# Query and key parts stored in the order of the stacks' rows by eight writes, and the attention maxima spread over experts 3 to 7

## The reference

```python
xn = _layernorm(x)
# L1 attention, 16 heads of 8
att = einsum('bhqd,bhkd->bhqk', q, k) / sqrt(8)
att = softmax(att)                      # needs the maximum of each row
out = einsum('bhqk,bhkd->bhqd', att, v) @ Wo.T + bo
# L1 mixture of experts: 8 experts (top 2 by a router) and a shared one
h = (x @ W1[e]) * silu(x @ W3[e]);  expert_out = h @ W2[e]
out = sum_e expert_out * w_full[e] + shared(x)
x = x + attention + experts
```

## Time and profile before

| | us |
|---|---|
| median of 3 runs | 2470.44 (2469.55 to 2471.82) |
| the profiled execution | 2469.61 |
| its span, first to last instruction | 2467.8 |
| PE busy | 1954.3 (79%) |
| DVE busy | 1303.0 (53%) |
| ACT busy | 731.4 (30%) |
| POOL busy | 309.3 (13%) |
| mean granted PE clock | 0.878 of full |

### The profile page before, as it was taken

How to read it: one execution, slowest core, us unless ns; L and a number is a source line. 1 busy time by engine, 2 the same in 40 slices (tenths; PEclk the granted TensorE clock), 3 DMA queues, 4 the chain that set the end, 5 groups by cost and what they waited for, 6 DMA issues and landing times.

```text
span 2467.8 us, 46598 instructions
## 1 busy us (share of the span) xinstructions
PE 1954.3 (79%) x19644; PEld 1120.4 (45%) x19644; DVE 1303.0 (53%) x3084; ACT 731.4 (30%) x1321; POOL 309.3 (13%) x242
## 2 busy tenths in 40 slices
PE   1887788778888788877888768888688877878777
PEld 1444444444454444534445435454344553445544
DVE  1555455554455554655546455555455554565544
ACT  0222242223522235122251232422233223423133
POOL 0110101102101021011110111101111102011020
PEclk9898898888988799878899789997899978989789
DMA  4000200002000020000200001000110002000010
GB/s 154 1 1 1 44 7 2 1 1 44 7 2 1 1 44 7 2 1 3 43 6 2 1 20 26 6 2 1 30 16 6 2 1 41 5 6 1 1 39 7
DMA packets 33762, 36.08 MB, mean 15 GB/s; under 512 B 3652, under 2 KB 32116, under 8 KB 33012
## 3 DMA queue, kind: packets, MB, share of 16 engines
q1 hardware_dynamic: 33556, 33.10, 6.2%
HBM read 24.44 MB, written 8.65 MB: 13 GB/s over the span
## 4 chain that ended last, share of the span: by engine, by line
PE 61%; DVE 26%; ACT 7%; issue 4%; POOL 1%; DMA 1%; SPq 1%; ACTq 0%; DVEq 0%
PE bank L831 6%; PE bank L846 5%; DVE amx L1428 5%; PE bank L935 4%; PE bank L657 4%; PE bank L856 3%; PE bank L563 3%; PE bank L691 3%; PE bank L603 3%; DVE lrec L1275 3%; DVE lmx L1261 2%; PE bank L796 2%; PE bank L678 2%; PE bank L614 2%; DVE fp L1214 2%
## 5 line engine op out<-in xcount | busy, mean ns | idle before, releaser
L1419 DVE TENSOR_TENSOR mh<-bank,silu 128x512 f32<-128x512 f32 x144 | 98.8, 690 | 232.2 <-PE bank L846 232.2
L1275 DVE RECIPROCAL lrec<-bank 128x256 f32<-128x256 f32 x64 | 112.3, 1755 | 144.0 <-PE bank L704 143.4
L441 POOL TENSOR_TENSOR lc<-lc,ls 128x512 f32<-128x512 f32 x32 | 41.0, 1280 | 1026.6 <-DVE lc L1236 1026.6
L1065 ACT ACTIVATE silu<-bank 128x512 f32<-128x512 f32 x144 | 85.1, 597 | 277.8 <-PE bank L831 277.8
L831 PE MATMUL bank<-xn2T,w_mw 128*128 128x512 f32 x288 | 164.8, 702 | 1.8
L1428 DVE TENSOR_REDUCE amx<-bank 128x2 f32<-128x512 f32 x256 | 155.0, 680 | 0.0
L603 PE MATMUL bank<-hT,w_wqkv 128*128 128x512 f32 x256 | 133.9, 666 | 23.5 <-ACT hT L967 17.3
L856 PEld LDWEIGHTS bank<-w_mw,mh 128*128 128x128 f32 x1152 | 136.7, 192 | 24.2 <-issue 24.2
L856 PE MATMUL bank<-w_mw,mh 128*128 128x128 f32 x1152 | 141.4, 277 | 0.0
L1261 DVE TENSOR_REDUCE lmx<-bank 128x4 f32<-128x512 f32 x128 | 79.5, 684 | 73.8 <-PE bank L657 73.8
L1016 ACT ACTIVATE lnmT<-bank 128x512 bf16<-128x512 bf16 x16 | 9.6, 597 | 348.2 <-PE bank L666 348.2
(11 more groups left out here) (260 smaller groups left out, 3821.9 us busy)
## 6 DMA issues: line engine op xcount, KB each, us to landing
dparts<-parts SPq DMA_DIRECT2D x8, 768.0 KB, 3.6
phi<-dparts SPq DMA_DIRECT2D x96, 64.0 KB
lc<-dparts SPq DMA_DIRECT2D x96, 64.0 KB
w_mw<-in_mw SPq DMA_DIRECT2D x3, 1152.0 KB
x_in<-in_x SPq DMA_DIRECT2D x8, 256.0 KB, 13.7
out<-res SPq DMA_DIRECT2D x8, 256.0 KB, 2.3
w_wqkv<-in_wqkv SPq DMA_DIRECT2D x1, 1536.0 KB
w_w<-in_w SPq DMA_DIRECT2D x1, 682.0 KB
```

The lines of the kernel that those rows point to most:

```text
L1275: V.reciprocal(lrec[:, k % 2, :], bank_of("loc_den", k)[:, 0:SEQ]).then_inc(sem["loc_rec"], 1)
L1419: V.tensor_tensor(mh[:, n % 4, :], bank_of("moe_u", n)[:], silu[:, n % 2, :], ALU.mult).then_inc(sem["moe_h"], 1)
```

## The change

Two edits.

First, `dparts` in device memory has the axes `[w, part, odd, d, h // 2, t]` instead of `[w, part, h, d, t]`. One part of one parity of heads is then one run of 64 KB in the order in which it goes into the stack: 8 rows (d) of 8 KB. The 24 reads keep their place, number and size, each with 8 runs of 8 KB where it had 64 runs of 1 KB. The write is cut into eight, one per pair of heads, each of 16 partitions x 6 runs of 1 KB, and SP waits for all eight (8 * 16 on the semaphore).

Second, `MAX_AT` spreads the 16 pairs over experts 3 to 7 as 2, 3, 3, 4, 4 instead of 5, 5, 6 over experts 5 to 7. The wait for the stacks moves with pair 0 from expert 5 to expert 3. Numbers of later lines grow by one.

```diff
-    "parts_out": 16, "stack_in": 26 * 16, "nm_out": 16, "nm_in": 32,
+    "parts_out": 8 * 16, "stack_in": 26 * 16, "nm_out": 16, "nm_in": 32,
...
-        dparts = nc.dram_tensor("dparts", [2, 3, AH, AD, T], BF16, kind="Internal").ap()
+        dparts = nc.dram_tensor("dparts", [2, 3, 2, AD, AH // 2, T], BF16, kind="Internal").ap()
...
-        MAX_AT = {5: range(0, 5), 6: range(5, 10), 7: range(10, 16)}
+        MAX_AT = {3: range(0, 2), 4: range(2, 5), 5: range(5, 8), 6: range(8, 12), 7: range(12, 16)}
...
-                sp.dma_start(dparts.rearrange("w s h d t -> (h d) w s t"), parts[:]).then_inc(sem["parts_out"], 16)
-                sp.wait_ge(sem["parts_out"], now("parts_out", 16))
+                for h in range(AH // 2):
+                    sp.dma_start(dparts[:, :, :, :, h, :].rearrange("w s o d t -> (o d) (w s) t"),
+                                 parts[2 * AD * h:2 * AD * h + 2 * AD].rearrange("p w s t -> p (w s) t")).then_inc(
+                                     sem["parts_out"], 16)
+                sp.wait_ge(sem["parts_out"], now("parts_out", 8 * 16))
...
-                            sp.dma_start(st_[r0:r0 + AD, :, :],
-                                         dparts[w_, part].rearrange("(h o) d t -> o d h t", o=2)[odd]).then_inc(
-                                             sem["stack_in"], 16)
+                            sp.dma_start(st_[r0:r0 + AD, :, :], dparts[w_, part, odd]).then_inc(sem["stack_in"], 16)
```

## The result

| | before | changed |
|---|---|---|
| median, us | 2470.96 (2469.55 to 2471.82, 4 runs) | 2515.28 (2513.64 to 2522.01, 4 runs) |
| ratio, 95% interval | | 1.019 (1.0178 to 1.0203) |
| the profiled execution, us | 2469.61 | 2522.01, span 2520.2 |

The changed kernel is 44 us slower, 5.5 us a turn. Its profiled execution is the longest of the four, 52 us or 6.6 us a turn above before, so what is read from it is a little more than what the median holds.

What follows compares the result with a forecast made beforehand. PE led the chain, with DVE the bound in experts with maxima. Per turn, 4.35 us wait plus 1.8 clock less 3.5 from maxima gave +2.65, +21 in eight turns: 2492 us, range 2442 to 2540.

Steps and rivals of the forecast that it cites:

- Maxima: Spreading pairs over experts 3 to 7: five experts take 38.33 us against 41.81, 3.5 us less a turn if stacks are there.
- The place of the loss: PE ahead of pair 0 in expert 3: waits 4.35 us for late stacks, then half clock; no later slack.
- The reads: Stack transfers: rate stays within 58 to 102 GB/s; stacks complete 22.75 us behind the write's issue, before the write term.
- the 21.3 us that were asked: Deadline for complete stacks, counted from the write's issue, with pair 0 in expert 3; before, PE asked at 32.7 us.
- some credit: Allowance for the reads' 8 KB runs: halfway from turn 1's 24.8 us to the best turn's 20.7.
- the row of the ones: Evidence against fast long runs: two reads of ones, 8 KB runs to two partitions, moved 28 GB/s together.
- reads in step: Rival, chance 0.08: long packets keep engines on the same 8 partitions, 56 to 60 GB/s, 2545 to 2565 us.
- The figure of 28 GB/s: Assumed rate shared by every 4 neighbouring SBUF partitions, giving a read to 8 partitions 56 GB/s, two overlapping reads 112.
- The write: Eight pieces instead of one land later: 2.9 us, the middle between 0.8 (issue) and 5 (16 partitions held to 112 GB/s).
- The clock: PE, idle while waiting, restarts at half clock: 1.8 us lost a turn, counted for 3.5 us of half speed.
- The long runs are fast: Rival, chance 0.16: reads reach 208 GB/s, become bound by issue, nothing waits, 2443 us.
- Late by little: Rival, chances 0.06 faster and 0.07 no measurable difference: stacks under 1.7 us late, 2444 to 2469 us.

Runs made afterwards that it cites:

- e7: Changed kernel's maxima; whole stacks in device memory, double parts written twice, writes started as each part is made, four reads of 48 partitions, 1 KB runs: 2442.18 us.
- e1: Changed kernel with the maxima back in experts 5 to 7, new layout and transfers kept: 2469.21 us beside 2469.16 for the kernel before.
- e2: Kernel before, old layout and one write, with the changed kernel's maxima over experts 3 to 7: 2492.73 us, ratio 1.0105 to the kernel before.
- e5: Changed kernel with eight useless products on PE ahead of its wait for the stacks: 2497.3 us, ratio 1.0117 to the kernel before.
- e3: Changed kernel with the 24 reads reordered so that q and k reads of the same partitions are neighbours: 2546.9 us, ratio 1.0305 to the kernel before.
- e6: Kernel before, old layout and one write, with maxima over experts 4 to 7 as 3, 4, 4, 5 pairs: 2444.22 us beside 2471.19.
- e9: e2 with the parts written by eight DMAs of 16 partitions into the old layout: 2506.76 us, ratio 1.0146 to the kernel before.

## Why the prediction was right in kind and wrong in size

**Maxima: right.** The costs of 6.84, 7.21 and 10.87 us for experts with three and four pairs and the last are 6.99, 7.39 and 10.88 us in the trace. The gain of 3.5 us a turn shows in e7, where nothing waits: 3.6 each by the medians, 3.2 in turn 1 from the gates of expert 3 to those of expert 8 (38.62 us).

**The place of the loss: right.** PE waits ahead of pair 0 for a DMA, nothing behind it gives the time back, and the clock falls to half. e1 shows that the loss is gone when only the time of asking is undone.

**The reads: the term that failed.** The sum gave them 22.75 us from the write's issue with the write of before, which is 19.15 us from the first read (22.75 - 3.6). The changed kernel takes 23.4, 4.25 more. Most of that was wrong before any new layout came in, as e2 shows: old write, old reads, and the stacks complete 25.8 us behind the write's issue, 22.2 from the first read. The trace of before agrees. Its record of the stacks' semaphore has the last increment 21.5 to 28.7 us behind the write's issue, 26.0 on average, and 26.1, 28.7 and 21.5 in the turns 1, 5 and 8, where I had read 24.8, 27.3 and 20.7 off the slices. In turn 1 I had taken off 1.2 us for x, and nothing was to be taken off. So in that trace the old transfers never met the 21.3 us that were asked, not even in turn 8.

Then I gave longer runs "some credit", halfway to the best turn. No row supported a credit, and the row of the ones spoke against it; none came. The misreading and the credit together are 3.05 us (25.8 - 22.75). What is left of the 4.25 us, 1.2, lies between 22.2 and 23.4, and may be the long runs or scatter. I had named reads in step as a rival (56 to 60 GB/s), with a chance of 0.08. The rate that came, 76 GB/s, lies between it and the forecast, and the old runs have the same rate in e2.

The figure of 28 GB/s for two engines on four partitions stood on one pair of packets, and isn't as firm as it looks. The pair right behind, of the same form, is recorded with 0.43 and 0.42 us, which makes 38 GB/s. The levels of 55 and 109 GB/s in e2's slices are the better support for 28 GB/s to each four partitions, and even they are an inference.

**The write: nearly right.** The term was +2.9 us between ends of 0.8 and 5. The first read went out 2.0 us later, 0.9 less than the term. The upper end was wrong in kind: the writes were spaced by their issue, 3.70 us for eight, and moved at 150 to 250 GB/s, not at 112.

```profile
GB/s 0 0 0 0 0 19 115 109 109 102 179 263 173 147 237 199 154 231 243 198 218 205 166 231 224 147 231 224 211 250 166 96 71 0 0 0 0 0 0 0
```

(The changed kernel, 268.6 to 275 us in 40 slices.)

**The clock: too small.** I took 1.8 us from the restart behind the transposes, which lasted 3.5 us. Here half clock lasts from 297.68 to about 303.5, and costs 2.8 us by e5's trace. The row that I used was a restart behind a shorter idle time, with work of another kind behind it. Why the clock takes longer here is not settled.

In sum for turn 1, from the gates of expert 3 to those of expert 8: 7.6 us for the wait and 2.8 for the clock, less the 3.2 that the maxima give, are 7.2 us. Measured are 335.05 - 285.95 = 49.10 us against 41.81, 7.3 more. Over whole turns that execution lost 6.6 us each, against the predicted 2.65. The median execution lost 5.5 us; its waits were not recorded. Of the 4.0 us by which that execution missed the forecast (6.6 - 2.65), the longer wait holds 3.3 (7.65 - 4.35; reads 4.25, write -0.9) and the clock 1.0; the small rest has the other sign.

**The rivals.** "The long runs are fast" had a chance of 0.16, and the 76 GB/s show that it was not so. "Late by little" did not come either. The Trainium skill's rule that a second DMA at partition 64 brings only 6% ("SBUF — State Buffer", section "Can I just issue two DMAs to hit both halves?") does not hold here as it stands: by my estimate two reads of 8 partitions that were in each other's way entirely would move 56 GB/s, and 76 to 102 were seen. Without the estimate, e3 says it too: with other neighbours the same reads took 26.9 us on average instead of 23.4, 15% more.

## What to carry to other kernels

Before moving a consumer forward, read from the trace when its data land, turn by turn, and count the lateness at full price with the clock on top; an edit to the transfers earns a credit only from a row of the very form that it makes. For DMAs into SBUF, ask first how many partitions one transfer reaches, and with them how many engines. Four reads of 48 partitions with 1 KB runs moved twice as fast as 24 reads of 8 partitions with 8 KB runs. With these transfers, whose writes also start as each piece is made, the same move of the maxima gained 29 us where it had lost 44; the share of either was not measured. The cheap half was at hand all the time: with the old transfers and pair 0 one expert later, nothing but `MAX_AT` changed, e6 gains 27 us, about 19 of them by the maxima. Read a landing from an experiment that asks early, or from the semaphore, and not from the last slice of a rate.

## What the hardware showed that I had not expected

- Packets eight times as long brought nothing to reads into 8 partitions: 76 GB/s with 8 KB, 74 with 1 KB in the same stretch of e2.
- The same 24 reads took 26.9 or 23.4 us on average by their order alone (28.0 or 23.4 in turn 1).
- The rate of the reads of before differs from turn to turn of one execution, 79 GB/s in turn 1 and a steady 102 in the last, and so do executions of e9, 2490 to 2515 us. The times of kernels that wait for these reads scatter; e1, with the changed kernel's transfers and no wait, stays within 2467 to 2472 us. Why an execution falls one way or the other stays open.
- Work of no use in an unavoidable wait of some microseconds paid: 18 us in eight turns (e5).
